# Two 16-head attentions: queries taken two tiles at a time, in every second step

## What is computed

```python
def _L2_xattn_ref(x_q, x_kv, attn_mask, key_padding_mask, Wq, Wk, Wv, Wo):
    q = (x_q @ Wq.T).reshape(b, tq, h, hd).transpose(0, 2, 1, 3)     # h = hd = 16
    k = (x_kv @ Wk.T).reshape(b, tk, h, hd).transpose(0, 2, 1, 3)    # tk = 77
    v = (x_kv @ Wv.T).reshape(b, tk, h, hd).transpose(0, 2, 1, 3)
    scores = jnp.einsum('bhqd,bhkd->bhqk', q, k) / jnp.sqrt(jnp.float32(hd))
    scores = jnp.where(key_padding_mask[:, None, None, :], -jnp.inf, scores + attn_mask)
    w = jax.nn.softmax(scores, axis=-1)
    out = jnp.einsum('bhqk,bhkd->bhqd', w, v)
    return out.transpose(0, 2, 1, 3).reshape(b, tq, d) @ Wo.T
...
x = x + jnp.tanh(g_xattn[2]) * _L2_xattn_ref(_layernorm(x, axis=-1), ctx_1024, mask_SxS2_ff0, mask_BxS2_bf0, ...)
x = x + jnp.tanh(g_xattn[3]) * _L3_xattn_ref(_layernorm(x, axis=-1), ctx_1024, ctx_1024, mask_1x1xSxS2_bk0, ...)
```

## Time and profile before

| | |
|---|---|
| median of 3 runs | 1948.39 us |
| the profiled execution | 1948.08 us |
| its span | 1946.1 us |
| PE busy | 1656.8 us (85%) |
| DVE busy | 1148.0 us (59%) |
| ACT busy | 886.7 us (46%) |
| mean granted clock of PE | 0.929 |

### The profile page before, as it was taken

How to read it: one execution, slowest core, us unless ns; L and a number is a source line. 1 busy time by engine, 2 the same in 40 slices (tenths; PEclk the granted TensorE clock), 3 DMA queues, 4 the chain that set the end, 5 groups by cost and what they waited for, 6 DMA issues and landing times. The chain is left out here.

```text
span 1946.1 us, 29978 instructions
## 1 busy us (share of the span) xinstructions
PE 1656.8 (85%) x10149; PEld 1254.6 (64%) x10149; DVE 1148.0 (59%) x2495; ACT 886.7 (46%) x1803; POOL 321.2 (17%) x359
## 2 busy tenths in 40 slices
PE   7895578896899997899997579999954999979998
PEld 5452245555677665588886269999944888854446
DVE  4765567676455556899887743322247889842115
ACT  2232567764443210365564345555544566533213
POOL 0000000000000001311100155555553111101110
PEclk9898799998899988999998779999977999979999
DMA  5001000002100000100001922222252000010002
GB/s 154 1 1 44 0 1 1 1 1 68 49 1 1 1 1 9 30 1 1 2 2 55 382 82 72 72 72 72 72 168 67 2 1 2 1 47 1 1 0 87
DMA packets 62845, 78.78 MB, mean 40 GB/s; under 512 B 13179, under 2 KB 52655, under 8 KB 62319
## 3 DMA queue, kind: packets, MB, share of 16 engines
q1 hardware_dynamic: 42967, 47.35, 7.4%
q0 software_dynamic: 7584, 20.72, 3.4%
q10 hardware_dynamic: 12152, 8.85, 1.5%
HBM read 58.16 MB, written 18.74 MB: 40 GB/s over the span
## 5 line engine op out<-in xcount | busy, mean ns | idle before, releaser
L2880 PEld LDWEIGHTS moe_bank<-moe_xt,moe_w1e 128*128 128x128 f32 x1264 | 155.0, 193 | 5.7 <-DVE moe_xt L2728 1.7
L2880 PE MATMUL moe_bank<-moe_xt,moe_w1e 128*128 128x128 f32 x1264 | 155.8, 277 | 1.1 <-DVE moe_xt L2728 1.1
L2890 PE MATMUL moe_bank<-moe_w,moe_xin 128*128 x632 | 149.3, 379 | 0.0
L2954 ACT ACTIVATE moe_xin<-moe_bank,moe_b 128x128 f32<-128x128 f32 x316 | 90.1, 368 | 125.8 <-PE moe_bank L2880 124.2
L390 PE MATMUL l0f_hb<-l0f_xt,l0f_w 128*128 128x512 f32 x256 | 126.0, 624 | 5.4 <-DVE l0f_a L321 3.8
L1092 POOL TENSOR_TENSOR all_x<-all_x,l1f_bias 128x256 f32 x32 | 23.1, 724 | 632.2 <-DVE l1f_xn L204 632.2
L2890 PEld LDWEIGHTS moe_bank<-moe_w,moe_xin 128*128 128x128 f32 x632 | 114.0, 190 | 12.3
L209 DVE BATCH_NORM_STATS2 all_stats<-all_x 128x6 f32<-128x256 f32 (+1 forms) x256 | 104.0, 422 | 8.4
L2737 DVE TENSOR_TENSOR moe_y<-moe_bank,moe_b2r 128x256 f32<-128x256 f32 x79 | 33.6, 425 | 119.0 <-PE moe_bank L2890 116.1
L2797 POOL DMA_INDIRECT moe_results<-moe_y,moe_row x79 | 78.0, 987 | 125.1 <-DVE moe_y L2737 121.1
L2728 DVE COPY moe_xt<-moe_bank 128x256 f32<-128x256 f32 x79 | 33.6, 425 | 106.2 <-PE moe_bank L2868 105.1
(11 more groups left out here) (478 smaller groups left out, 3812.1 us busy)
## 6 DMA issues: line engine op xcount, KB each, us to landing
moe_w<-in_L_ffn_W SPq DMA_DIRECT2D x32, 512.0 KB, 10.3
moe_w<-moe_results SPq DMA_DIRECT2D x16, 512.0 KB, 8.8
all_x<-in_x SPq DMA_DIRECT2D x4, 1024.0 KB, 13.1
out_x<-all_x SPq DMA_DIRECT2D x8, 512.0 KB, 2.9
l0f_w<-in_L_ffn_w_T SPq DMA_DIRECT2D x2, 1024.0 KB, 6.4
moe_inputs<-moe_xin ACTq DMA_DIRECT2D x8, 256.0 KB, 7.3
moe_inputs<-moe_w1e ACTq DMA_DIRECT2D x8, 256.0 KB, 7.5
moe_b2r<-in_L_ffn_b SPq DMA_DIRECT2D x1, 2048.0 KB, 14.0
```

The costliest lines, as they stand in the source:

```text
L2880: ins = nc.tensor.matmul(out, w1e[:, at:at + P], xt[:, u, c * P:(c + 1) * P], start=(c == 0), stop=(c == DC - 1))
L2890: ins = nc.tensor.matmul(bank[4 + u][:, 0:D], ht[:, u, c * P:(c + 1) * P], w2[:, ds(e * (HC * D) + c * D, D)], start=(c == 0), stop=(c == ...
L2954: ins = nc.scalar.activation(ht[:, u, m * P:(m + 1) * P], bank[1 + u][:, m * P:(m + 1) * P], ACT.Gelu, bias=b1[:, ds(e * HC + m, 1)])
```

## The change

A step now takes either two tiles through `turn`, `copy_x`, `query` and `copy_q`, or none. These parts return at once where `u` is 1, the odd tiles; where `u` is 0 they do their own tile and the next. Since they are issued three steps ahead, they fall on the steps with odd s. `turn` has four transposes that fill all 512 columns of `x_bank`, `copy_x` is one copy of 512 columns, `query` has four products of 256 columns that write over the whole bank, and `copy_q` has two copies of 256 columns. `xn` grows to four tiles, `xt` is one tile of two halves instead of two, and `norm` is issued five steps ahead instead of four.

```diff
-        xn = s.sb("xn", [P, AHEAD, D])
-        xt = s.sb("xt", [P, AHEAD, D])
+        xn = s.sb("xn", [P, 2 * AHEAD, D])
+        xt = s.sb("xt", [P, DC, 2 * P])
...
                 def norm(t, u):
-                    dve.wait_ge(s.xt_ps, ev(t, back=2))
-                    normalise(nc, sh, xn[:, u, :], t).then_inc(s.xn_ready, 1)
+                    if t >= 2 * AHEAD:
+                        dve.wait_ge(s.xt_ps, ev(t, back=4))
+                    normalise(nc, sh, xn[:, t % (2 * AHEAD), :], t).then_inc(s.xn_ready, 1)
...
-                unrolled(T, [(scale_o, 0), (norm, 4), (first_keys, 3), (first_values, 2), (masked_scores, 2), (shift(0), 2), (update, 0), (shift(1), 2),
+                unrolled(T, [(scale_o, 0), (norm, 5), (first_keys, 3), (first_values, 2), (masked_scores, 2), (shift(0), 2), (update, 0), (shift(1), 2),
...
                 def turn(t, u):
-                    pe.wait_ge(s.xn_ready, ev(t))
+                    if u:
+                        return
+                    pe.wait_ge(s.xn_ready, ev(t + 1))
                     pe.wait_ge(s.q_ready, ev(t, back=1))
-                    for c in range(DC):
-                        ins = nc.tensor.transpose(x_bank[:, c * P:(c + 1) * P], xn[:, u, c * P:(c + 1) * P], sh.ident[:, :])
-                    ins.then_inc(s.xt_ps, 1)
+                    for v in range(2):
+                        for c in range(DC):
+                            ins = nc.tensor.transpose(x_bank[:, (c * 2 + v) * P:(c * 2 + v + 1) * P],
+                                                      xn[:, (t + v) % (2 * AHEAD), c * P:(c + 1) * P], sh.ident[:, :])
+                    ins.then_inc(s.xt_ps, 2)
 
                 def query(t, u):
-                    pe.wait_ge(s.xt_ready, ev(t))
+                    if u:
+                        return
+                    pe.wait_ge(s.xt_ready, ev(t + 1))
...
-                            ins = nc.tensor.matmul(x_bank[:, D + m * P:D + (m + 1) * P], wq[:, k, m * P:(m + 1) * P],
-                                                   xt[:, u, k * P:(k + 1) * P], start=(k == 0), stop=(k == DC - 1))
-                    ins.then_inc(s.q_ps, 1)
+                            ins = nc.tensor.matmul(x_bank[:, m * 2 * P:(m + 1) * 2 * P], wq[:, k, m * P:(m + 1) * P],
+                                                   xt[:, k, :], start=(k == 0), stop=(k == DC - 1))
+                    ins.then_inc(s.q_ps, 2)
...
                 def copy_x(t, u):
-                    act.wait_ge(s.xt_ps, ev(t))
-                    act.wait_ge(s.q_ps, ev(t, back=2))
-                    nc.scalar.activation(xt[:, u, :], x_bank[:, 0:D], ACT.Copy).then_inc(s.xt_ready, 1)
+                    if u:
+                        return
+                    act.wait_ge(s.xt_ps, ev(t + 1))
+                    act.wait_ge(s.q_ps, ev(t, back=1))
+                    nc.scalar.activation(xt[:, :, :], x_bank[:, :].rearrange("p (c n) -> p c n", c=DC), ACT.Copy).then_inc(s.xt_ready, 2)
...
-                    act.wait_ge(s.q_ps, ev(t))
-                    act.wait_ge(s.s_ps, ev(t, back=2))
+                    act.wait_ge(s.q_ps, ev(t + 1))
+                    act.wait_ge(s.s_ps, ev(t, back=1))
                     for m in range(DC):
-                        ins = nc.scalar.activation(qt[:, u, m * P:(m + 1) * P], x_bank[:, D + m * P:D + (m + 1) * P],
+                        ins = nc.scalar.activation(qt[:, :, m * P:(m + 1) * P],
+                                                   x_bank[:, m * 2 * P:(m + 1) * 2 * P].rearrange("p (v n) -> p v n", v=2),
                                                    ACT.Identity, bias=bq[:, m:m + 1])
-                    ins.then_inc(s.q_ready, 1)
+                    ins.then_inc(s.q_ready, 2)
```

## The result

The changed kernel takes 1977.32 us (median of 4 runs, 1976.47 to 1978.09), the kernel before on the same chip 1948.36 us. The ratio is 1.0151, with a 95% interval of 1.0134 to 1.0169: slower by 1.5%, some 29 us. The forecast was 1981 in a range of 1971 to 1988. The profiled execution took 1976.47 us.

A forecast was written before the change was run, and what follows sets the result against it. PE's list and DVE's chain were both taken to bound a step. Per attention 14.1 (steady part) + 2.34 (first steps) = 16.45 us, 32.9 for two, on 1948.08: 1981 us, range 1971 to 1988.

The forecast's parts named there:

- What bounds the kernel: In a 7.11 us attention step, PE's list and DVE's chain both end within 0.05 us of the next L2404.
- Long interval: L2404 to L2404 with the pair's turn and query: 7.11 + 0.22 + 0.85 = 8.18 us.
- transposes: Two more transposes in turn in each step that takes a pair, 0.11 us each, fully on the path: +0.22.
- width: Query's eight records of 256 columns instead of 128 take 1.74 us instead of 0.89: +0.85.
- Short interval: L2404 to L2404 without turn and query: DVE sets it at 7.11 us, so a plain one gives back nothing.
- steady part: Attention behind its first steps: 14 intervals with a pair add 15.0, less 0.8, together +14.1 us per attention.
- short steps with context: Steps with context transposes but no turn or query, j = 4, 12, 20: 7.34 against 7.55 us, -0.21 each.
- Rival 4: Norm is hidden in steps without turn and query, which take 6.90 us; total 1976.5, chance 0.08.
- First steps: Start of each attention: the first two queries come later and last longer, 1.28 + 1.06 = +2.34 us.
- Elsewhere: Norm a step earlier, POOL's bias add, DVE's busy time and ACT's saved fixed cost: nothing added to the total.
- Rival 1: Wide products in query are cheap, bound by weight load: query grows only 0.18 us; total 1960, chance 0.06.
- Rival 3: PE idle in steps without turn and query lets the clock fall, up to 48 us; ending near 2029, chance 0.05.

The follow-up runs named there:

- e_neither: Kernel before, with turn, copy_x, query and copy_q left out for all tiles but the first two: 1926.43 us, ratio 0.9927.
- b_order: Kernel before, same instructions reordered: DVE's norm behind update, PE's scores before turn and output before query, ACT's copies to match: 1935.72 us, ratio 0.9946.
- e_split: Changed kernel with the pair's query and copy_q split in halves, one half in each step: 1950.33 us, ratio 1.0016.
- e_turn_pairs: Changed kernel with query and copy_q per tile in every step again, only turn and copy_x in pairs: 1950.6 us, ratio 1.0037.
- e_norm_late: Changed kernel with DVE's norm issued behind update instead of behind scale_o: 1977.09 us, ratio 1.0183.
- e_early: Changed kernel with ACT's copy_x of the second pair issued before the exps of tile 0: 1971.15 us, ratio 1.0137.
- b_order2: b_order with POOL's key blocks moved from steps 3 and 5 of a batch to 6 and 7: 1935.84 us, ratio 0.9962.

## Why the prediction was right, and where its sizes were off

**What bounds the kernel.** Right in the main: PE's list and DVE's chain each nearly fill a step, the long interval shows PE's (8.13) and e_neither DVE's (7.00). The reading of the 7.11 missed two things. The first: PE's list came to the next L2404 "with no visible wait", but the row at 894.30 shows 0.40 us of waiting for ACT's copy. It is the same before and after, so it is not in the sum; it is room on PE, which the order of b_order uses. The second is the third path: scores start at 2.74, behind turn's two transposes, masked_scores 0.94 after them, and 3.43 later come the products, which is 7.11. It is the 6.90 of the earlier trace rows and twice 0.11. With four transposes it gives 7.34, as e_split and e_turn_pairs show, with none 6.90. So turn holds the step through DVE, and its place ahead of scores matters.

**Long interval, 8.18.** Measured 8.13. The terms for transposes (0.22: scores at 2.96 instead of 2.74) and width held (query to output 1.73, where 0.89 + 0.85 = 1.74 was forecast), so the growth is 1.07 as said. It starts from PE's own path, 7.06, and not from 7.11, since in the step before PE still waited 0.05 for update.

**Short interval, 7.11.** Measured 7.00; this is the term of the steady part that was mis-sized. I let masked_scores follow 0.42 after norm's start, as in the earlier trace rows. But there masked_scores was also held by scores, 0.94 after theirs. With the scores earlier it starts 897.31 - 896.99 = 0.32 after norm's start, 0.08 before norm's recorded end. From the sums to masked_scores it is 0.95, and 3.42 from there to the products as before. The short steps with context came as forecast (7.33, said 7.34). About 11 plain short intervals at -0.11 are 1.2 of the 2.0 to 2.4 us by which the steady part came out under 14.1; 14 long ones at -0.05 are 0.7. In the fourth layer the kernel before had also lost 0.67 us in its first interval (7.79 instead of 7.12) to the clock's fall of the earlier trace rows.

**Rival 4** (norm fully hidden, 6.90) did not occur by itself. In e_norm_late it did, where norm was moved.

**First steps, 2.34.** Measured 4.18 and 3.77. The mechanism was as described: the wait for the value copy grew (2.80 on DVE) and the second query started 1.5 us later, as said (13.25 instead of 11.72 after the first transposes). What the sum lacked is the clock: after 2.69 us of waiting the query took 3.64 us instead of 1.89, which is 1.75 of the gap between 4.18 and 2.34. I had named this as part of the range with at most 1.7 us for one drop; that it comes in both attentions I had not expected. In the fourth layer it cost less against before, since there a drop already stood (0.57; first steps of 14.80 instead of 14.43). e_early, without the wait, shows the query's weight loads at 1.59 again.

**Elsewhere, 0.** The traces have -3.3 us outside the two stages: -1.2 ahead of the third layer's, +0.3 between them, -2.4 behind the fourth's. What the last is was not tried. In the twelve traces the stretch behind the fourth's attention lasts from 219.5 to 222.7 us, over code that is the same in all, so it lies within the spread of single runs.

**Rivals 1 and 3.** Rival 1 (width nearly free, 1960) falls by the rows of L2367: 1.73 us for eight records is 0.216 each against 0.111 before, a factor of 1.95. The figures of the Trainium skill's page "TensorE: Matmul & The Clock Gate", section "Back-to-back issue gap", are then not those of these f32 products. Rival 3 falls for the steady part: with a wait of 0.71 us in every second step the granted clock stayed at 1.00 over 140 us.

Over both attentions the steady part is 23.8 instead of 28.2, the first steps 7.9 instead of 4.7, and elsewhere, which is what is left of the span, -3.3 instead of 0: 1981 - 4.4 + 3.2 - 3.3 = 1976.5, which is the profiled execution. These are three errors of about equal size that partly cancel. The mechanism was right; that the total came within 5 us is in part luck: the two falls of the clock, which stood in the range and not in the sum, make up for most of what the steady part lacked.

## What to carry to other kernels

Where two engines each need nearly the whole of a step, work gathered into every second step costs the gathered amount there and returns only the distance to the other engine's limit; here that was 0.11 us of 1.1. Wider products and copies are worth what their rows save (0.06 us per pair on PE, and ACT wasn't short of time), so price them before paying with balance. And to win at such a double limit all the paths have to be shortened in the same step, also one that crosses from engine to engine: b_order did, by order alone, and is 0.5% faster than the kernel before.

## What the runs showed of the hardware

- Two elementwise operations of 128x616 with two SBUF inputs, one on POOL and one on DVE, lengthen each other when they overlap: 1.22 to 1.84 us on POOL, 0.79 to 1.81 on DVE. Each has the length of its wait in its own record, and no idle time is shown before it. The step grew by 0.5 to 0.6 (8.57 to 9.11 in e_norm_late, 7.33 to 7.95 from b_order2 to b_order).
- The granted clock fell after a wait of PE of 2.69 us (0.66 over 5 us) and the eight records of 256 columns took 3.64 us instead of 1.89. After the shorter wait before the change, 2.07 us on PE in both, it was 1.00 in the third layer's attention and 0.57 in the fourth's; and in e_early it fell in the fourth (0.57 over 4 us) behind waits of 0.92 and 0.47. So in these traces the length of the wait alone does not decide.
- A DVE instruction that needs nothing of the one ahead starts about 0.08 us before that one's recorded end (897.31 against 897.39). A chain summed from recorded lengths comes out too long by that for each such pair.
